# Full attention prepared during the layer norm, its first operands split by VectorE; the local blocks' residual added sequence by sequence

## The chip, the cores and the metric

The kernel runs on one core of a Trainium2 chip, in one launch. The metric is the device time of the launch in microseconds, lower is better, and the median of several runs is compared. The engines are TensorE (PE: matmuls, with its weight loads shown as PEld), VectorE (DVE), ScalarE (ACT), GpSimd (POOL) and SyncE (SP, which issues most transfers here). TensorE has a granted clock with two levels, 1.2 and 2.4 GHz, which the profile shows as 0.50 and 1.00.

## The reference

The input x has 4 sequences of 512 tokens with 128 features. Two "layers" of a macaron network are applied to it:

```python
x = x + 0.5 * _L0_ffn_ref(_layernorm(x))     # 8 gated experts
x = x + _L0_attn_ref(_layernorm(x))          # linear attention, 16 heads of 64
x = x + 0.5 * _L0_ffn_ref(_layernorm(x))     # the experts again
x = x + 0.5 * _L1_ffn_ref(_layernorm(x))     # 6 x (local attention, window 32; gated feed-forward)
x = x + _L1_attn_ref(_layernorm(x))          # full attention, 16 heads of 8, two sets of keys
x = x + 0.5 * _L1_ffn_ref(_layernorm(x))     # the six local layers again
```

The full attention takes queries, keys, second keys (`W_K_prime`) and values from the normalised x, forms `softmax(q k^T / sqrt(8)) v` for both sets of keys over all 512 tokens of a sequence, and mixes the two results with `alpha` and `1 - alpha` before the output projection. The 0.5 of the fourth and the sixth line is the "residual" of this case: half of what the six local layers give is added to x.

## The kernel before

Everything stays on chip, features on the 128 partitions: `M.x` is [128, 4 x 512]. The program is a sequence of blocks, and the order of instructions within a block is written out by hand for each engine. A block ends with a barrier of all engines (the lines L93 and L502 in the trace), after which the engines branch into the next block. The blocks around the change are, in order: `loc0` (the six local layers), the layer norm `ln4`, the full attention, the layer norm `ln5`, and `loc1` (the six local layers again).

**Local block.** It walks over 96 tiles of 128 tokens (6 layers x 4 sequences x 4 tiles) in a software pipeline: in step `n` each engine works on tiles `n`, `n-1`, ... down to `n-9`, and nine further steps (`for n in range(9): step(DEPTH, n, ...)`) drain it. The feed-forward output of a whole sequence is added to the working copy `zs` in step `n-9` of its last tile by `add_ffn` (L1255 for the lower 64 partitions, L1258 for the upper 64, which are shifted by one token). Of the last layer, sequence 0 is added at step 12 of layer 5, and sequences 1, 2 and 3 at steps 0, 4 and 8 of the drain. `rescale` (L1241) starts the feed-forward of the next sequence. `maximum` (L1205) starts the softmax of a tile. After the drain, VectorE adds `0.5 * zs` to `M.x` in two instructions over all four sequences (L1322, L1324).

**Layer norm.** `layernorm_block` computes means with matmuls against a constant (L107), subtracts (DVE L138), squares (ACT L132), forms the variance (PE L112), takes the inverse square root by a table-free guess and three Newton steps on VectorE (L66 to L75), spreads it by matmuls (L118) and multiplies (DVE L147) into `M.xh`. SyncE and GpSimd have no work in `ln4`.

**Full attention.** It walks over 16 groups `u` (4 sequences x 4 groups of four heads), 16 slots each; `K` counts the slots, and `begins(K, offset)` says whether group `u` has its step of that offset in slot `K`. Ahead of the slots stand: three transfers by SyncE (L1405 to L1407: the weights `wqkk`, `wv_full`, `wo_full`), a memset of `lowest` on GpSimd (L1551), and on VectorE two memsets of `V`, five tiny instructions for the two mixing coefficients, and three instructions that fold signs and the scale into `wqkk` (L1579 to L1593). TensorE and ScalarE wait for all of this. The first slots (K = -16 to -10) then project values (L1457, four matmuls against one PSUM bank) and queries, keys, second keys (L1465) of group 0. Each of these three is copied to `plain` by ScalarE (L1538, L1540), and is split into operands for the fast matmul format: VectorE cuts low bits (`high`, L1610), GpSimd multiplies by a sign column (`rest`, L1559) and adds the two (`qkk`, L1563). There are two buffers of `plain`, `high` and `rest`. In slot K = 0 the score matmuls (L1441) of group 0 start, once all three operands are there (`split_ready`); VectorE reduces each pair of banks to a maximum (L1601).

## Time and profile before

| | |
|---|---|
| time, median of 3 runs | 4337.57 us (4336.9 to 4341.59) |
| the profiled execution, its own time | 4342.59 us |
| its span, first to last instruction | 4340.8 us |
| PE busy | 4033.6 us, 93% |
| DVE busy | 3357.6 us, 77% |
| POOL busy | 2965.1 us, 68% |
| ACT busy | 2587.4 us, 60% |
| `loc0` ends, `ln4` ends, full attention ends | 2186.9, 2206.7, about 2710 us |

A busy share is a mean over the whole span, so it says nothing of a seam between two blocks, where one engine works and the others wait. Such places are read from the timeline: a row has the start, the time in microseconds, the engine, the line, what is written from what, the shapes, and in brackets how long the engine sat idle before and what released it.

### The profile page before, as it was taken

The page shows a single profiled execution, that of the slowest core. Times are in us where ns is not written, and L with a number is a line of the kernel's source. Part 1 is how long each engine was busy: PE and PEld are TensorE (multiplying, and loading weights), DVE is VectorE, ACT ScalarE, POOL GpSimd, SP SyncE. Part 2 cuts the span into 40 slices and gives each one's busy share as a digit, 9 for nine tenths or more (in the row PEclk, how much of TensorE's full clock was granted, in tenths as well). Part 3 has the DMA queues.
Part 4 walks back from the last instruction along what each step waited for, and adds up shares of the span by engine and source line. Part 5 has one row for each costly group of instructions (what it writes and reads, how often), then busy time and mean ns, then how long its engine had stood idle before and what let it go on. Part 6 is the DMA issues. An engine that isn't in the chain of part 4 may idle for free. (4 is left out here: it accounts for less than half of the span.)

```text
span 4340.8 us, 151604 instructions
## 1 busy us (share of the span) xinstructions
PE 4033.6 (93%) x66856; PEld 2965.1 (68%) x66856; DVE 3357.6 (77%) x3997; ACT 2587.4 (60%) x3022; POOL 2965.1 (68%) x3501
## 2 busy tenths in 40 slices
PE   8989969999999999999968888799999999999997
PEld 5655557877777777887633332577877887777775
DVE  5635568887888888888658884689888888887885
ACT  4424436666666667666527775367666666666664
POOL 2202158988888888888524441688888888888884
PEclk9999989999999999999969997899999999999999
DMA  4304233233233323322100000332323333232221
GB/s 150 124 10 143 105 94 82 75 88 82 75 88 80 83 78 84 90 69 74 40 11 1 1 1 1 105 86 78 85 78 85 88 84 87 72 88 78 73 67 38
DMA packets 169726, 316.94 MB, mean 73 GB/s; under 512 B 39336, under 2 KB 43056, under 8 KB 166640
## 3 DMA queue, kind: packets, MB, share of 16 engines
q1 hardware_dynamic: 153520, 241.18, 20.5%
q0 software_dynamic: 15552, 66.07, 4.9%
q8 instruction: 529, 8.67, 0.9%
q14 instruction: 125, 1.02, 0.1%
HBM read 92.03 MB, written 20.05 MB: 26 GB/s over the span
## 5 line engine op out<-in xcount | busy, mean ns | idle before, releaser
L684 PE MATMUL psum<-loc_w_hl,loc_z_lo 128*128 128x512 f32 x1152 | 508.5, 441 | 36.1 <-DMA loc_w_hl<-parted 25.9
L1069 POOL TENSOR_TENSOR loc_rc_k<-loc_rc_k,loc_rs_k 128x1024 f32<-128x1024 f32 x192 | 454.5, 2367 | 18.9 <-DVE loc_rs_k L1197 18.9
L1183 DVE TENSOR_REDUCE loc_ssq<-loc_sq 128x16 f32<-128x1024 f32 x384 | 463.9, 1208 | 3.4 <-POOL loc_rn L1065 3.3
L930 ACT ACTIVATE loc_sq<-psum 128x1024 f32<-128x1024 f32 x192 | 197.0, 1026 | 444.1 <-PE psum L686 439.0
L1069 POOL TENSOR_TENSOR loc_rc_q<-loc_rc_q,loc_rs_q 128x1024 f32<-128x1024 f32 x192 | 459.3, 2392 | 0.0
L686 PE MATMUL psum<-loc_w_hl,loc_z_hi 128*128 128x512 f32 x1152 | 455.3, 395 | 1.8 <-issue 1.8
L685 PE MATMUL psum<-loc_w_hl,loc_z_hi 128*128 128x512 f32 x1152 | 454.3, 394 | 2.5 <-issue 2.5
L1087 POOL TENSOR_TENSOR loc_prob<-loc_prob,loc_recip 128x1024 f32<-128x1024 f32 x192 | 365.9, 1906 | 97.2 <-DVE loc_recip L1220 96.6
L781 PE MATMUL psum<-loc_PT,loc_V 64*64 64x32 f32 x24576 | 404.8, 220 | 10.4 <-issue 10.2
L781 PEld LDWEIGHTS psum<-loc_PT,loc_V 64*64 64x64 f32 x24576 | 381.2, 135 | 35.6 <-issue 12.4
L801 PEld LDWEIGHTS psum<-loc_outT,loc_wo 128*128 128x128 f32 x3072 | 378.5, 194 | 17.8 <-issue 1.5
L1075 POOL TENSOR_TENSOR loc_qk_q<-loc_rc_q,loc_rn 128x1024 f32<-128x1024 f32 x192 | 366.0, 1906 | 27.0 <-issue 1.3
L1178 DVE TENSOR_TENSOR loc_rc_q<-psum,loc_rot 128x1024 f32<-128x1024 f32 x192 | 234.8, 1223 | 193.3 <-ACT loc_sq L925 160.4
L801 PE MATMUL psum<-loc_outT,loc_wo 128*128 128x128 f32 x3072 | 380.2, 278 | 0.0
L1075 POOL TENSOR_TENSOR loc_qk_k<-loc_rc_k,loc_rn 128x1024 f32<-128x1024 f32 x192 | 367.3, 1913 | 12.0
L755 PEld LDWEIGHTS psum<-loc_kT,loc_qT 64*32 64x32 f32 x24576 | 270.7, 105 | 134.5 <-issue 132.7
L960 ACT ACTIVATE loc_PT<-psum 128x1024 f32<-128x1024 f32 x192 | 197.0, 1026 | 260.7 <-PE psum L691 260.7
L755 PE MATMUL psum<-loc_kT,loc_qT 64*32 64x64 f32 x24576 | 310.8, 226 | 43.3 <-issue 42.9
L1522 ACT ACTIVATE full_probT<-psum 128x512 f32<-128x512 f32 x512 | 272.4, 598 | 120.8 <-PE psum L1448 120.8
L384 DVE TENSOR_TENSOR moe_hid<-moe_hid,moe_spread 128x512 f32<-128x512 f32 x256 | 218.3, 869 | 153.5 <-ACT moe_hid L298 142.7
L1601 DVE TENSOR_REDUCE full_least<-psum 128x2 f32<-128x1024 f32 x256 | 305.9, 1219 | 28.9 <-PE psum L1441 23.5
L1205 DVE TENSOR_REDUCE loc_negmax<-psum 128x16 f32<-128x1024 f32 x192 | 234.4, 1221 | 108.5 <-PE psum L755 107.0
(199 smaller groups left out, 9753.3 us busy)
## 6 DMA issues: line engine op xcount, KB each, us to landing
loc_V<-loc_V SPq DMA_DIRECT2D x1152, 128.0 KB
loc_V<-loc_V SPq DMA_DIRECT2D x672, 64.0 KB
loc_w_hl<-parted POOLq DMA_DIRECT2D x72, 512.0 KB, 4.3
parted<-moe_halves POOLq DMA_DIRECT2D x18, 1024.0 KB, 5.2
moe_spread<-moe_gates SPq DMA_DIRECT2D x64, 256.0 KB, 4.1
moe_raw<-in_wqkv POOLq DMA_DIRECT2D x18, 512.0 KB, 6.0
moe_w<-in_moe_w SPq DMA_DIRECT2D x32, 256.0 KB, 3.3
loc_wo<-in_wo SPq DMA_DIRECT2D x12, 512.0 KB, 4.8
```

Of the source, the lines that this page charges most:

```text
L684: pe.matmul(M.bank[bank + g], z_lo[:, r, tokens], w[:, 0, cols], start=True, stop=False)
L685: pe.matmul(M.bank[bank + g], z_hi[:, r, tokens], w[:, 1, cols], start=False, stop=False)
L686: mm = pe.matmul(M.bank[bank + g], z_hi[:, r, tokens], w[:, 0, cols], start=False, stop=True)
L755: mm = pe.matmul(M.bank[YB + c][q:q + 32, p * 64:(p + 1) * 64], qT[r:r + 64, p, q:q + 32], kT[r:r + 64, p, k0:k0 + 64], start=False, stop= ...
L781: mm = pe.matmul(M.bank[WB + c][64 * j:64 * j + 64, m * P + q:m * P + q + 32], V2[r:r + 64, b, w, p * 64:(p + 1) * 64], PT[r:r + 64, p, q: ...
L801: mm = pe.matmul(M.bank[ZB][:, 0:P], wo[:, p, :], outT[:, p // (PAIRS // 2), p % (PAIRS // 2), :], start=(p == 0), stop=(p == PAIRS - 1))
L1069: pool.tensor_tensor(rc, rc, rs[:, :], ALU.add).then_inc(added, 1)
L1075: pool.tensor_tensor(pair_major(out[:, :, :, :]), by_pair(rc), spread_heads(rn[:, a:a + HEADS], DH), ALU.mult).then_inc(ready, 1)
L1087: pool.tensor_tensor(both, both, spread_heads(recip[:, :], 2 * WINDOW), ALU.mult).then_inc(p_ready, 1)
L1183: dve.tensor_reduce(ssq[:, a:a + HEADS], heads(sq[:, :]), AX_X, ALU.add).then_inc(totalled, 1)
L1522: act.activation(probT[:, (u * 8 + y * 4 + kb) % SETS, r, :], B[B_BANKS[n % 3]], ACT.Exp).then_inc(b_free, 1)
L1601: dve.tensor_reduce(least[:, u % 2, i, 2 * (k % 2):2 * (k % 2) + 2, y], M.psum[:, b:b + 2, :], AX_X, ALU.max, negate=True).then_inc(a_free, 1)
```

## The change

Four things are changed.

1. The three weight transfers, the memsets, the coefficients and the folding of `wqkk` move from the head of the full attention into the layer norm block `ln4` ahead of it: SyncE issues the transfers there, and GpSimd does all the rest (VectorE's part too).
2. The value projection moves from offset `PROJECT - 2` to `PROJECT + 6`, behind the three projections of its group, on TensorE and ScalarE.
3. For group 0 alone, VectorE does GpSimd's two steps of the split (`rest` and the sum) as well; GpSimd splits from group 1 on.
4. In both local blocks the residual is added to `M.x` right behind each sequence's last `add_ffn`, in two instructions of 512 columns for each sequence, instead of two of 2048 columns at the end.

```diff
@@ layernorm_block (called with full=A for ln4)
+        if full is not None:
+            @block.sync
+            def _(sp):
+                sp.dma_start(M.f_wqkk[:, :, :], full["wqkk"].rearrange("p (y n) -> p y n", y=3)).then_inc(M.f_loaded, 16)
+                sp.dma_start(M.f_wv[:, :], full["wv_full"]).then_inc(M.f_loaded, 16)
+                sp.dma_start(M.f_wo[:, :], full["wo_full"]).then_inc(M.f_loaded, 16)
+
+            @block.gpsimd
+            def _(pool):
+                pool.wait_ge(M.full_loaded, 16 * M.full_dmas)
+                pool.tensor_scalar(M.f_other[:, :], M.sel[:, SUM_ROW:SUM_ROW + 1], -1.0, 1.0, ALU.mult, ALU.add).then_inc(M.f_folded, 1)
...
+                pool.memset(M.f_lowest[:, :, :, :], 0.0).then_inc(M.f_prepared, 1)
+                pool.memset(M.f_V[:, :, :, :, AD + 1:32], 0.0).then_inc(M.f_prepared, 1)
+                pool.memset(M.f_V[:, :, :, :, AD:AD + 1], 1.0).then_inc(M.f_prepared, 1)
...
+                pool.wait_ge(M.f_loaded, 48)
+                for y, cols, factor in ((0, slice(0, 2 * AD), AD ** -0.5), (0, slice(2 * AD, 3 * AD), -AD ** -0.5),
+                                        (slice(1, 3), slice(AD, 2 * AD), -1.0)):
...
+                    pool.tensor_scalar(w, w, factor, None, ALU.mult).then_inc(M.f_prepared, 1)
+                pool.wait_ge(M.f_prepared, 7)
@@ local block, add_ffn
+                if L * SEQS + s >= (DEPTH - 1) * SEQS:
+                    x_out = M.x[:, r * T:(r + 1) * T]
+                    dve.wait_ge(z_ffn, upto_seq(L, s))
+                    dve.scalar_tensor_tensor(out=x_out[0:64], in0=zs[0:64, r, 0:T], scalar=0.5, in1=x_out[0:64],
+                                             op0=ALU.mult, op1=ALU.add)
+                    dve.scalar_tensor_tensor(out=x_out[64:P], in0=zs[64:P, r, 1:T + 1], scalar=0.5, in1=x_out[64:P],
+                                             op0=ALU.mult, op1=ALU.add).then_inc(x_added, 1)
@@ local block, behind the drain
-            dve.wait_ge(z_ffn, upto_seq(DEPTH, -1))
-            x_out = M.x[:, :].rearrange("p (s n) -> p s n", n=T)
-            dve.scalar_tensor_tensor(out=x_out[0:64], in0=zs[0:64, :, 0:T], scalar=0.5, in1=x_out[0:64],
-                                     op0=ALU.mult, op1=ALU.add)
-            dve.scalar_tensor_tensor(out=x_out[64:P], in0=zs[64:P, :, 1:T + 1], scalar=0.5, in1=x_out[64:P],
-                                     op0=ALU.mult, op1=ALU.add).then_inc(x_added, 1)
@@ full_attention_block, schedule and PE, ACT
-    FIRST, LAST = PROJECT - 2, SLOTS * GROUPS + OUT - SLOTS + 1
+    FIRST, LAST = PROJECT, SLOTS * GROUPS + OUT - SLOTS + 1
-            u = begins(K, PROJECT - 2)
+            u = begins(K, PROJECT + 6)
-            pe.wait_ge(M.full_loaded, 16 * M.full_dmas)
-            pe.wait_ge(prepared, 6)
-            pe.wait_ge(v_loaded, 16)
-            pe.wait_ge(out_loaded, 16)
@@ full_attention_block, gpsimd
-            pool.memset(lowest[:, :, :, :], 0.0).then_inc(prepared, 1)
-                    if u is not None:
+                    if u:
@@ full_attention_block, vector (the memsets, coefficients and folds at its head are gone)
                         dve.tensor_scalar(high[:, m % 2, :].bitcast(I32), plain[:, m % 2, :].bitcast(I32), LOW_BITS, None,
                                           ALU.bitwise_and).then_inc(cut, 1)
+                        if u == 0:
+                            sign = SIGNS + (y > 0)
+                            dve.tensor_scalar(rest[:, m % 2, :], plain[:, m % 2, :], M.sel[:, sign:sign + 1], None,
+                                              ALU.mult).then_inc(parted, 1)
+                            dve.wait_ge(cut, m + 1)
+                            dve.wait_ge(parted, m + 1)
+                            dve.tensor_tensor(qkk[:, u % KEPT, y, :], high[:, m % 2, :], rest[:, m % 2, :],
+                                              ALU.add).then_inc(split_ready, 1)
```

What stands on VectorE between the end of `ln4` (the last two branches) and the first score maximum (`full_least`), before the change:

```order
L147 TENSOR_TENSOR xh_late<-xh_late,psum 128x512 x4
L93 UNCONDITIONAL_BRANCH
L1576 UNCONDITIONAL_BRANCH
L1579 MEMSET full_V 128x128x23
L1580 MEMSET full_V 128x128
...
L1593 TENSOR_SCALAR full_wqkk<-full_wqkk 128x16x16
L1593 TENSOR_SCALAR full_wqkk<-full_wqkk 128x16x8
L1593 TENSOR_SCALAR full_wqkk<-full_wqkk 128x32x8
L1610 TENSOR_SCALAR full_high<-full_plain 128x512 x3
L1601 TENSOR_REDUCE full_least<-psum 128x2 x4
```

and with the change (line numbers are those of the changed kernel):

```order
L178 TENSOR_TENSOR xh_late<-xh_late,psum 128x512 x4
L93 UNCONDITIONAL_BRANCH
L1597 UNCONDITIONAL_BRANCH
L1614 TENSOR_SCALAR full_high<-full_plain 128x512
L1618 TENSOR_SCALAR full_rest<-full_plain,sel 128x512
L1622 TENSOR_TENSOR full_qkk<-full_high,full_rest 128x512
...
L1605 TENSOR_REDUCE full_least<-psum 128x2 x4
```

(the three rows of the split stand there three times). The preparation is gone from the head of the block, and six instructions have come into the split. The preparation stands now on GpSimd, between the end of `loc0` and the end of `ln4`, where it had no instruction before:

```order
L137 UNCONDITIONAL_BRANCH
L140 TENSOR_SCALAR full_other<-sel 128x1
...
L143 MEMSET full_lowest 128x1024
L144 MEMSET full_V 128x128x23
L145 MEMSET full_V 128x128
...
L156 TENSOR_SCALAR full_wqkk<-full_wqkk 128x16x16
L156 TENSOR_SCALAR full_wqkk<-full_wqkk 128x16x8
L156 TENSOR_SCALAR full_wqkk<-full_wqkk 128x32x8
L93 UNCONDITIONAL_BRANCH
L93 ISA
```

The end of a local block on VectorE, here of `loc1`, from sequence 2's `add_ffn` (its two instructions write `zs`) to the end, before the change:

```order
L1255 SCALAR_TENSOR_TENSOR zs<-psum,loc_vec,zs 64x512
L1258 SCALAR_TENSOR_TENSOR zs<-psum,loc_vec,zs 64x512
L1241 TENSOR_TENSOR loc_xn<-loc_xc,psum 128x512
L1248 SCALAR_TENSOR_TENSOR loc_gg<-psum,loc_vec,loc_gg 128x512 x2
...
L1258 SCALAR_TENSOR_TENSOR zs<-psum,loc_vec,zs 64x512
L1322 SCALAR_TENSOR_TENSOR x<-zs,x 64x2048
L1324 SCALAR_TENSOR_TENSOR x<-zs,x 64x2048
```

and with the change:

```order
L1286 SCALAR_TENSOR_TENSOR zs<-psum,loc_vec,zs 64x512
L1289 SCALAR_TENSOR_TENSOR zs<-psum,loc_vec,zs 64x512
L1295 SCALAR_TENSOR_TENSOR x<-zs,x 64x512
L1297 SCALAR_TENSOR_TENSOR x<-zs,x 64x512
L1272 TENSOR_TENSOR loc_xn<-loc_xc,psum 128x512
L1279 SCALAR_TENSOR_TENSOR loc_gg<-psum,loc_vec,loc_gg 128x512 x2
```

Sequence 2's residual stands now ahead of `loc_xn`, which starts sequence 3's feed-forward; the two wide instructions at the end are replaced by two such narrow ones for sequence 3.

## Rows read from the trace of the kernel before

**Rows 1.** Timeline from the end of `loc0` to the first scores.
```profile
2182.28 2.28 DVE L1322 SCALAR_TENSOR_TENSOR x<-zs,x 64x2048 f32<-64x2048 f32 x1
2184.57 2.29 DVE L1324 SCALAR_TENSOR_TENSOR x<-zs,x 64x2048 f32<-64x2048 f32 x1
2188.09 5.38 PE L107 MATMUL psum<-x,mean_w 128*128 128x512 f32 x8 [7.40 <-PEq L502]
...
2197.20 0.17 DVE L68 TENSOR_SCALAR ln_rstd<-ln_var 128x16 int32<-128x16 int32 x1
...
2205.97 0.69 DVE L147 TENSOR_TENSOR xh_late<-xh_late,psum 128x512 f32<-128x512 f32 x1 [0.45 <-PE psum L118]
2207.37 0.34 SPq L1405 DMA_DIRECT2D full_wqkk<-in_wqkk  x1
2207.37 0.95 POOL L1551 MEMSET full_lowest<- 128x1024 f32 x1 [43.66 <-POOLq L93]
...
2208.05 2.51 DVE L1579 MEMSET full_V<- 128x2944 f32 x1 [1.40 <-PEq L93]
...
2213.35 2.05 PE L1457 MATMUL psum<-full_wv,xh_late 128*128 128x128 f32 x8 [7.42 <-DMA full_wo<-in_wo_full]
...
2215.19 4.55 PE L1465 MATMUL psum<-xh_late,full_wqkk 128*128 128x512 f32 x6
...
2217.14 0.60 ACT L1538 ACTIVATE full_plain<-psum 128x512 f32<-128x512 f32 x1 [1.02 <-PE psum L1465]
...
2217.84 1.82 POOL L1559 TENSOR_SCALAR full_rest<-full_plain,sel 128x512 f32<-128x512 f32 x1 [9.52 <-ACT full_plain L1538]
2217.85 0.45 DVE L1610 TENSOR_SCALAR full_high<-full_plain 128x512 int32<-128x512 int32 x1 [4.79 <-ACT full_plain L1538]
...
2225.79 1.26 POOL L1563 TENSOR_TENSOR full_qkk<-full_high,full_rest 128x512 fp32r<-128x512 f32 x1
...
2227.11 0.80 PE L1441 MATMUL psum<-full_qkk 32*128 32x512 f32 x4 [7.37 <-POOL full_qkk L1563]
```

**Rows 2.** Timeline and stages (windows) where the expert block follows `ln2`.
```profile
332.07 0.69 DVE L147 TENSOR_TENSOR xh_early<-xh_early,psum 128x512 f32<-128x512 f32 x1 [0.43 <-PE psum L118]
...
333.51 3.59 PE L262 MATMUL psum<-xh_early,wg 128*8 128x512 f32 x8 [1.48 <-PEq L93]
...
333.00:338.00 5.00, 3.59 (x8) 0.66 (x8) 1.97 (x4) 1.71 (x3) 2.30 (x2) 1.00 0.64 203
```

**Rows 3.** Windows: us, busy (count) of PE, PEld, DVE, ACT, POOL; granted clock; DMA share, GB/s.
```profile
2208.00:2209.00 1.00, 0.00 (x0) 0.00 (x0) 0.95 (x1) 0.00 (x0) 0.32 (x1) 0.80 0.79 113
...
2265.00:2270.00 5.00, 4.41 (x28) 1.40 (x24) 4.02 (x5) 3.07 (x7) 1.70 (x2) 0.84 0.02 3
...
2300.00:2320.00 20.00, 18.74 (x122) 7.30 (x116) 17.05 (x21) 15.52 (x31) 10.08 (x8) 1.00 0.00 1
```

**Rows 4.** Single lines: durations min/median/max in ns, first and last start.
```profile
L384 DVE TENSOR_TENSOR moe_hid<-moe_hid,moe_spread x256: 675/692/2818, 45.8 to 536.8; 128x512 f32<-128x512 f32 x128
L1188 DVE TENSOR_SCALAR loc_ssq<-loc_ssq x192: 169/676/2046, 587.6 to 4265.1; 128x32 f32<-128x32 f32 x192
```

**Rows 5.** Timeline of the drain of `loc1`.
```profile
4279.94 0.76 DVE L1258 SCALAR_TENSOR_TENSOR zs<-psum,loc_vec,zs 64x512 f32<-64x512 f32 x1
...
4281.90 1.22 DVE L1205 TENSOR_REDUCE loc_negmax<-psum 128x16 f32<-128x1024 f32 x1 [1.21 <-PE psum L755]
...
4312.72 0.76 DVE L1258 SCALAR_TENSOR_TENSOR zs<-psum,loc_vec,zs 64x512 f32<-64x512 f32 x1
4313.51 0.69 DVE L1241 TENSOR_TENSOR loc_xn<-loc_xc,psum 128x512 f32<-128x512 f32 x1
```

**Rows 6.** Sequence 0's `add_ffn` in `loc1`: timeline and a window.
```profile
4219.88 1.23 DVE L1197 TENSOR_TENSOR loc_rs_q<-psum,loc_rot 128x1024 f32<-128x1024 f32 x1
...
4231.33 1.23 DVE L1178 TENSOR_TENSOR loc_rc_q<-psum,loc_rot 128x1024 f32<-128x1024 f32 x1 [1.52 <-ACT loc_sq L925]
...
4204.00:4268.00 64.00, 63.43 (x1339) 51.77 (x1340) 53.79 (x65) 43.72 (x44) 53.57 (x67) 1.00 0.27 72
```

More of the change, by code:

```diff
@@ L87, in stage_semaphores, with layernorm_block @@
     return sem
-def layernorm_block(nc, M, src, dst, name, shifted=None):
+def layernorm_block(nc, M, src, dst, name, shifted=None, full=None):
     WIDE = 32
@@ L1319, in _, with full_tensors, full_attention_block @@
                 step(DEPTH, n, lambda t: t < 0)
-            dve.wait_ge(z_ffn, upto_seq(DEPTH, -1))
-            x_out = M.x[:, :].rearrange("p (s n) -> p s n", n=T)
-            dve.scalar_tensor_tensor(out=x_out[0:64], in0=zs[0:64, :, 0:T], scalar=0.5, in1=x_out[0:64],
-                                     op0=ALU.mult, op1=ALU.add)
-            dve.scalar_tensor_tensor(out=x_out[64:P], in0=zs[64:P, :, 1:T + 1], scalar=0.5, in1=x_out[64:P],
-                                     op0=ALU.mult, op1=ALU.add).then_inc(x_added, 1)
-def full_attention_block(nc, M, W):
+def full_tensors(nc, ctx, M):
+    sb = lambda n, s: ctx.enter_context(nc.sbuf_tensor(f"full_{n}", s, F32))
+    sem = lambda n: ctx.enter_context(nc.semaphore(f"early_{n}"))
+    M.f_coefs, M.f_other = sb("coefs", [P, 2]), sb("other", [P, 1])
+    M.f_wqkk = sb("wqkk", [P, 3, 4 * P])
+    M.f_wv, M.f_wo = sb("wv", [P, D]), sb("wo", [P, 4 * D])
+    M.f_lowest = sb("lowest", [P, 2, TILES, P])
+    M.f_V = sb("V", [P, 2, TILES, AH, 32])
+    M.f_loaded, M.f_prepared, M.f_folded = (sem(n) for n in ("loaded", "prepared", "folded"))
+def full_attention_block(nc, M):
     GROUPS = 4 * SEQS
@@ L1333, in full_attention_block @@
     PROJECT = -14
[L1334 removed]
+    FIRST, LAST = PROJECT, SLOTS * GROUPS + OUT - SLOTS + 1
     SETS, KEPT = 4, 4
[L1336 removed]
+    HI, SELECTED, SIGNS = 3 * AD, 0, 2
     with ExitStack() as ctx:
@@ L1450, in _ @@
                                   skip_group_check=True).then_inc(b_full, 1)
-                u = begins(K, PROJECT - 2)
+                u = begins(K, PROJECT + 6)
                 if u is not None and u % 4 == 0:
@@ L1522, in _ @@
                         act.activation(probT[:, (u * 8 + y * 4 + kb) % SETS, r, :], B[B_BANKS[n % 3]], ACT.Exp).then_inc(b_free, 1)
-                u = begins(K, PROJECT - 2)
+                u = begins(K, PROJECT + 6)
                 if u is not None and u % 4 == 0:
@@ L1720, in program @@
             M.xh = late.enter_context(nc.sbuf_tensor("xh_late", [P, NTOK], F32))
-            layernorm_block(nc, M, M.x, M.xh, "ln4")
-            full_attention_block(nc, M, A)
+            with ExitStack() as wide:
+                full_tensors(nc, wide, M)
+                layernorm_block(nc, M, M.x, M.xh, "ln4", full=A)
+                full_attention_block(nc, M)
             layernorm_block(nc, M, M.x, M.xh, "ln5", M.zs)
```

53 lines of the change are left out of this document (14 added, 39 removed).

## The prediction

> **What bounds the kernel now.** The change touches two kinds of seam, so I read the timeline there first, then the waits, then the stages around them. At the head of the full attention [rows 1] every engine waits for one chain. `ln4` ends with VectorE's L147 at 2205.97 + 0.69 = 2206.66. Weights are asked for at 2207.37 and the last of them releases TensorE only at 2213.35. The value projection takes TensorE until 2215.19, when the query projection starts; ScalarE has its result at 2217.14. Then the split of three operands runs through GpSimd, 1.82 us for the first product and 1.26 us for the last sum, and the first score matmul starts at 2227.11. Between end of `ln4` and first scores lie 20.45 us, and TensorE idles for 7.42 and 7.37 of them. Nothing comes into this stage from outside afterwards: all sixteen groups follow from group 0, so what group 0 gains the whole stage gains.
>
> The second seam is the end of each local block: the last `add_ffn` is followed by two instructions of 2.28 and 2.29 us, from 2182.28 to 2186.86 = 4.58 us, with no other engine at work, and `ln4` begins behind them [rows 1]. It is there twice.
>
> **The change, part by part.**
>
> *Preparation moved into `ln4`.* SyncE's transfers start about 20 us earlier. They took 2213.35 - 2207.37 = 5.98 us from the first issue to the last landing [rows 1]; `ln4` lasts from 2186.86 to 2206.66 = 19.8 us, so they are hidden. GpSimd gets a memset of 1024 columns (0.95 us, the row of L1551), one of 2944 (VectorE took 2.51; at GpSimd's rate of 1024 in 0.95 it is 2.7), a small one, five tiny ones, and behind the landed weights three products of 256, 128 and 256 columns. At the rate of L1559, 1.82 for 512, these are together 2.3 us. Sum: start at about 2187.6, tiny ones and memsets until 2193, weights there at 2193.5, products until about 2196. It ends 10 us ahead of `ln4`'s end and 1 us ahead of the Newton chain (L68 at 2197.20). Cost: nothing. If that cover were gone, each of the three products could hold up a VectorE instruction by its own length, 0.9 us at most.
>
> *TensorE's start.* With nothing to wait for but the barrier, it begins as it does where the expert block follows `ln2` [rows 2]: L147 ends at 332.76 and the matmul starts at 333.51, 0.75 us later. The seam behind `loc0` gives the other bound: 2186.86 to 2188.09, 1.23 us. I take 0.75, since the block ahead is the same layer norm: start at 2207.41 on the clock of the old trace, against 2215.19, so 7.78 us earlier. The value projection that stood ahead of it goes behind and fills part of a wait.
>
> *Clock.* At 2207.41 the clock is still granted in full: in 2208 to 2209 it reads 0.80, and TensorE had been idle since 2206 [rows 3]. Where `ln2` hands over in the same way the clock reads 1.00 from 333 to 338, and eight matmul records took 3.59 us, 0.45 each [rows 2]. A projection is two records, so the first is ready after 2 x 0.45 + 0.2 of latency = 1.1 us in place of 2217.14 - 2215.19 = 1.95. Were the clock at its lower level, it would be 1.95 again; both are kept.
>
> *The split on VectorE.* ScalarE copies in 0.60; VectorE starts 0.11 later (2217.85 against 2217.74). It then needs for each of three operands `high` 0.45, `rest`, and the sum. `rest` is a one-operand instruction of 512 columns like `high`: 0.45, or 0.69 if it runs at the rate of L147; I take 0.45. The sum has two SBUF operands, median 0.69 [rows 4]. With 0.05 for the waits on its own results that is 1.6 per operand. ScalarE's copies of the second and third operand are hidden behind it: the projections come every 0.9 us. Sum: 1.1 + 0.6 + 0.11 + 3 x 1.6 + 0.06 = 6.7 us from the start of the query projection to the first scores, where it was 2227.11 - 2215.19 = 11.92. Gain 5.2 us. With the lower clock 0.85 to 1.1 less (the third projection then comes after 5.2 us); with the slower `rest` 0.7 less.
>
> So the first scores start at 2214.1 in place of 2227.11: **13.0 us** earlier. Bounds: 13.0 - 1.1 - 0.7 - 0.5 (barrier) = 10.7, and 13.3 if the two-step instructions overlap their ends. The value projections of sequences 1 to 3 move by eight slots within the running stage; the work is the same, and I set them at nothing, with half a microsecond either way each.
>
> L1188, a VectorE instruction of 32 columns, has a least time of 169 ns and a median of 676 [rows 4], so VectorE does wait for something beside a working GpSimd. The Trainium skill (SBUF — State Buffer, Who interferes with whom) names it: a VectorE instruction in a two-port mode, or with two SBUF operands while GpSimd reads SBUF, takes a shared port in turns with GpSimd, the later one waiting for the whole instruction. That rule speaks against the preparation in `ln4`. By it the three products could each hold up one Newton step if they came 1 us later than worked out, and the sum would be 2.7 us less.
>
> *The residual.* Four pairs of 64x512 replace one pair of 64x2048. One instruction costs 0.69 us by the two-operand row [rows 4], a pair 1.4 with its wait. I place each pair:
> - Sequence 3: it is all that is left at the end. 4.58 - 1.4 = 3.2 us gained.
> - Sequence 2: in the drain, L1258 ends at 4313.48 and `rescale` L1241 starts at 4313.51, with no idle time; everything to the end hangs on it [rows 5]. The pair now stands between them. 1.4 us lost.
> - Sequence 1: L1258 ends at 4280.70 and VectorE idles 1.21 us until TensorE's scores let L1205 start at 4281.90 [rows 5]. The pair fits but for 0.2 us, and that softmax has slack. Nothing; 1.4 if the cover is gone.
> - Sequence 0: in the full pipeline, ahead of L1197 at 4219.88. VectorE's next idle time, 1.52 us ahead of L1178 at 4231.33, absorbs 1.4; TensorE is busy 63.43 of 64 us there, so it sets the pace and VectorE has slack [rows 6]. Nothing; 1.4 if not.
>
> Net 3.2 - 1.4 = 1.8 us per block, **3.6 us** for both; bounds 0.8 (sequence 0 exposed in both) and 4.0.
>
> **Sum.** 13.0 + 3.6 = 16.6 us. On the profiled execution's own time, 4342.59, that is 4326.0. That execution is 5.0 us above the median of the runs, so against the median: 4337.57 - 16.6 = 4321.0, or 0.38% less. Bounds of the terms alone: 10.7 + 0.8 = 11.5 and 13.3 + 4.0 = 17.3 us, that is 4326.1 to 4320.3; with the 2 us by which three runs' medians may differ (their own spread is 4.7), 4328 to 4318.
>
> **The rivals.** A difference within 0.2%, 8.7 us, is about what a measurement of this kernel can't tell from none.
>
> *The clock carries over.* The projections of group 1 run among group 0's first slots, at the lower level. TensorE will now idle for only about 3 us ahead of the first scores (from the end of the value projection, 2207.4 + 2.7 + 1.1 = 2211.2, to 2214.1), in place of 7.37. If the clock survives that, three projections take 1.1 in place of 1.95 each, in slots where TensorE had no idle time: 2.6 us more, and if it stays up until the old rise in 2265 to 2270 [rows 3], a few more. Time: 4321.0 - 2.6 to - 6 = 4315 to 4318.4. Against it: in 2208 to 2209 the full level was lost after an idle time of this length. For it: more work now lies close together ahead of the gap.
>
> *A wait takes the place of the one removed.* TensorE's new start is in a block whose code no engine has run yet; VectorE's first instruction in that block came only at 2208.05, 1.39 us behind L147, while SyncE and GpSimd had begun at 2207.37 [rows 1]. If every engine pays something of this kind, or the preparation disturbs `ln4`, or sequence 0's pair costs both blocks 1.4 us, 4 to 8 us of the gain are lost: 4325 to 4329.
>
> *It doesn't do what it says.* The operands come earlier, but the gain is less than 8.7 us: that needs the split on VectorE to take 4 us more than worked out, as if each `rest` or sum ran at more than twice its row's median. The two-operand row has a maximum of 2818 ns, yet that was beside a working GpSimd, which is idle here. Time: 4329 to 4338.
>
> *Slower.* The one mechanism that is large enough is the clock of the full attention's body. At the full level TensorE is busy 18.74 of 20 us [rows 3]; the same work at the lower level would take up to 37.5, so each microsecond at the lower level costs up to 0.47. The rise in 2265 to 2270 came when TensorE had hardly idle time. Were it delayed by a disturbance in the new order (the value projections now stand in the middle of a group), the change would be slower from 16.6 / 0.47 = 35 us more at the lower level on, and clearly so from 54: 4346 or more. Nothing speaks for a delay of this length, since the order of the first 35 slots is otherwise the same.
>
> **How the numbers follow.** Forecast 0.62; clock carried over 0.13; a wait in its place 0.13; doesn't do what it says 0.08; slower 0.04. The predicted time is the forecast's, 4321.0. For 8 in 10 the range takes the first three with their ends: 4315 to 4329. Faster by over 0.2% are the first three but for the last edge of the third, 0.86; within 0.2%, 0.11; slower by over 0.2%, 0.03.
>
> **What would show it.** Right: the first query projection within 1.3 us of L147's end, at the full clock; no wait for `full_wo`; first scores 7 to 8 us behind `ln4`'s end (20.45 before); GpSimd's last weight product over 8 us ahead of that end; one pair of `x<-zs,x` 64x512 at the end of each local block, 1.4 us long, and one directly ahead of `loc_xn` of sequence 3; sequence 0's pair with TensorE's busy share unchanged. Wrong: an idle time of TensorE of over 1.5 us behind the barrier; `ln4` longer than 19.8 us; VectorE's split beyond 5.5 us; a rise of the clock in the full attention more than 45 us behind its first scores (2227 to 2266 before), which would cost, or less than 30, which would give.

## The result, and the profile after

The changed kernel takes 4303.62 us (median of 6 runs, 4293.63 to 4315.7) beside 4338.4 for the kernel before on the same chip (6 runs, 4332.78 to 4346.0): ratio 0.9927, 95% interval 0.9906 to 0.9949. A second job gave 0.9939 (0.9918 to 0.9960). On 4337.57 these are 31.7 and 26.5 us, so about 29 us in place of the 16.6 predicted (the two medians of the first job lie 34.8 us apart, within its interval), and the time lies below the range. The profiled execution's own time is 4293.63 us, the fastest of the six, its span 4291.8.

The head of the full attention in the timeline of the changed kernel, against [rows 1]; columns as there:

```profile
2168.35 0.43 SPq L134 DMA_DIRECT2D full_wv<-in_wv_full  x1
2169.31 2.55 POOL L144 MEMSET full_V<- 128x2944 f32 x1
2173.85 2.29 POOL L156 TENSOR_SCALAR full_wqkk<-full_wqkk 128x256 f32<-128x256 f32 x3 [1.38 <-DMA full_wo<-in_wo_full]
2177.11 0.17 DVE L68 TENSOR_SCALAR ln_rstd<-ln_var 128x16 int32<-128x16 int32 x1
2184.53 0.69 DVE L178 TENSOR_TENSOR xh_late<-xh_late,psum 128x512 f32<-128x512 f32 x1 [0.20 <-PE psum L118]
2185.98 2.81 PE L1489 MATMUL psum<-xh_late,full_wqkk 128*128 128x512 f32 x6 [1.48 <-PEq L93]
2187.11 0.60 ACT L1560 ACTIVATE full_plain<-psum 128x512 f32<-128x512 f32 x1 [12.34 <-PE psum L1489]
2187.74 0.43 DVE L1614 TENSOR_SCALAR full_high<-full_plain 128x512 int32<-128x512 int32 x1 [2.52 <-ACT full_plain L1560]
2188.08 0.48 DVE L1618 TENSOR_SCALAR full_rest<-full_plain,sel 128x512 f32<-128x512 f32 x1
2188.63 1.05 PE L1481 MATMUL psum<-full_wv,xh_late 128*128 128x128 f32 x8
2188.67 0.69 DVE L1622 TENSOR_TENSOR full_qkk<-full_high,full_rest 128x512 fp32r<-128x512 f32 x1
...
2191.74 0.69 DVE L1622 TENSOR_TENSOR full_qkk<-full_high,full_rest 128x512 fp32r<-128x512 f32 x1
2192.48 0.80 PE L1465 MATMUL psum<-full_qkk 32*128 32x512 f32 x4 [2.80 <-DVE full_qkk L1622]
2193.32 1.23 DVE L1605 TENSOR_REDUCE full_least<-psum 128x2 f32<-128x1024 f32 x1 [0.89 <-PE psum L1465]
```

The reader is to see that every step stands where it was put. The weights land inside `ln4`, and GpSimd's last product ends at 2176.14. VectorE's chain of small instructions starts 0.8 us later (L66 at 2176.90), and the first Newton instruction shown (L68) still takes 0.17. `ln4` ends at 2185.22, the first query projection starts 0.76 behind it, six matmul records take 2.81 (0.47 each), and the first scores come 7.26 us behind `ln4`'s end, where it was 20.45. The seam gives 13.2 us; 13.0 was predicted.

The windows from the first maximum (L1605, L1601 before) to the first output, and from there to the last output of the full attention, of the changed kernel, then of the kernel before; columns as in [rows 3]:

```profile
2193.32:2262.40 69.08, 56.31 (x288) 20.03 (x288) 61.41 (x64) 36.42 (x67) 28.24 (x20) 0.86 0.00 0
2262.40:2660.80 398.40, 347.94 (x2226) 127.81 (x2226) 305.66 (x333) 279.96 (x527) 140.34 (x102) 0.97 0.00 1
```

```profile
2227.95:2302.40 74.45, 62.63 (x288) 21.63 (x288) 62.51 (x65) 36.69 (x67) 28.20 (x20) 0.74 0.00 1
2302.40:2706.30 403.90, 354.50 (x2226) 129.40 (x2226) 305.43 (x333) 279.94 (x527) 139.85 (x102) 0.95 0.00 1
```

The counts are the same and VectorE, ScalarE and GpSimd are as long busy, yet the stretches are 5.4 and 5.5 us shorter. What differs is the granted clock. It has two levels, 1.2 and 2.4 GHz, so 0.74 over 74.45 us is 2 x 0.26 x 74.45 = 39 us at the lower one; 0.86 over 69.08 us is 19 by the same sum, and 20 when added up over windows of 2 us, as all such times below. In the second stretch it is 44 and 25 us, in the changed kernel all of it in the drain behind the last scores. This is what the prediction's sum has no term for. Windows of the changed kernel around the place where the level comes back to stay:

```profile
2189.00:2193.00 4.00, 1.20 (x11) 0.78 (x9) 3.21 (x7) 1.17 (x2) 0.00 (x0) 0.94 0.01 2
2193.00:2198.00 5.00, 3.69 (x12) 1.08 (x8) 3.49 (x3) 0.57 (x1) 0.00 (x0) 0.50 0.00 0
...
2218.00:2221.00 3.00, 2.85 (x12) 1.46 (x11) 1.80 (x3) 2.27 (x3) 1.57 (x1) 0.70 0.00 0
2221.00:2226.00 5.00, 4.53 (x28) 1.50 (x26) 5.00 (x7) 4.80 (x10) 4.23 (x4) 1.00 0.00 0
```

The level falls with the first scores: 0.94 up to 2193, then 0.50. It comes back once, falls again, and rises for good 27 to 28 us behind the first scores (2192.48), where it was 39 to 41 ([rows 3] against 2227.11).

The last rows of VectorE in `loc1`, against [rows 5]:

```profile
4264.69 0.74 DVE L1286 SCALAR_TENSOR_TENSOR zs<-psum,loc_vec,zs 64x512 f32<-64x512 f32 x1 [2.94 <-PE psum L889]
4265.45 0.76 DVE L1289 SCALAR_TENSOR_TENSOR zs<-psum,loc_vec,zs 64x512 f32<-64x512 f32 x1
4266.25 0.68 DVE L1295 SCALAR_TENSOR_TENSOR x<-zs,x 64x512 f32<-64x512 f32 x1
4266.94 0.69 DVE L1297 SCALAR_TENSOR_TENSOR x<-zs,x 64x512 f32<-64x512 f32 x1
4267.66 0.69 DVE L1272 TENSOR_TENSOR loc_xn<-loc_xc,psum 128x512 f32<-128x512 f32 x1
```

Sequence 2's pair stands ahead of `rescale`, with no idle time between, for 1.4 us, as predicted. The last pair of the block takes 1.42 where 4.58 stood.

The two profiled executions are 48.0 us apart at VectorE's last instruction. The full attention (end of `ln4` to last output) has 499.7 - 475.6 = 24.1 of them, and the other 24 lie in everything else, where only 3 to 4 were expected. So one pair of profiles doesn't tell what the change is worth; the experiments had to.

### The profile page after: what moved, and what is told of

Read it like the earlier page. It is cut to its first block and busy times, and to the rows that moved or that the text cites. A ratio compares the mean times of both kernels' runs of the same rounds, so it can differ in the third digit from the quotient of the medians.

```text
span 4291.8 us, 151611 instructions
## 1 busy us (share of the span) xinstructions
PE 4005.3 (93%) x66856; PEld 2945.8 (69%) x66856; DVE 3375.6 (79%) x4005; ACT 2587.5 (60%) x3022; POOL 2963.9 (69%) x3505
## 5 line engine op out<-in xcount | busy, mean ns | idle before, releaser
L1605 DVE TENSOR_REDUCE full_least<-psum 128x2 f32<-128x1024 f32 x256 | 305.9, 1219 | 19.9 <-PE psum L1465 15.1
```

Source lines behind the costliest of these rows:

```text
L1605: dve.tensor_reduce(least[:, u % 2, i, 2 * (k % 2):2 * (k % 2) + 2, y], M.psum[:, b:b + 2, :], AX_X, ALU.max, negate=True).then_inc(a_free, 1)
```

## The experiments

The expectations below come from another count of the time at the lower level: their 46 (or 45), 34 and 20.5 us behind the first maximum are 39, 28 and 20 in the windows of the profile, their 95 and 58 for the full attention 98 and 60.

Each job shares its runs of the kernel before. Its median was 4338.4, 4336.6, 4325.8, 4334.9, 4327.2 and 4329.6 us from job to job, and in the four jobs with 23 runs or more of it the middle 8 in 10 of the 122 single runs went from 4320 to 4345. Times are therefore read as ratios within a job; a ratio of 0.9977 is 10 us.

**The parts, and both kernels again.** `resid_only` has the per-sequence residual alone, `full_only` the preparation, the moved value projection and the split on VectorE, with the old residual.

> The kernel before once more, unedited. Ratio 1.000. Its profile tells how far the local layers and the first linear stages move from one execution to the next, and whether the lower clock in the first 39 us of the full attention (2227 to 2266) is there every time: theory B says yes, theory A has no view.

> The changed kernel once more, unedited, for its own spread. Its median beside the kernel before is asked first: theory A (only the seams changed: 16.6 us) puts it near 4321 and the measured 4303.6 down to luck of the runs; theory B (the seams plus something systematic) near 4304. In its profile the first scores should again start 7.3 us behind the end of the layer norm. Where the profiles of two runs of one kernel differ in stages that the edit doesn't touch, that difference belongs to the run.

> The kernel before with the residual alone added sequence by sequence. Prediction's sum: 3.6 us less (ratio 0.9992), bounds 0.8 to 4.0. Rival: the residual's pairs change the running pipeline of the local blocks and give the unexplained rest, some 18 us (ratio 0.995).

> The changed kernel with the old residual at the end of each local block: preparation in the layer norm, value projection behind, split on VectorE. Prediction's sum: 13.0 us less (ratio 0.997). Rival, the clock: with an earlier rise in the full attention 18 to 28 us less (ratio 0.9935 to 0.996). If the residual carries the rest, 13.

| | median us | ratio | 95% interval |
|---|---|---|---|
| before_again | 4335.55 | 1.0003 | 0.9982 to 1.0024 |
| after_again | 4310.56 | 0.9939 | 0.9918 to 0.9960 |
| resid_only | 4319.83 | 0.9964 | 0.9944 to 0.9984 |
| full_only | 4311.46 | 0.9942 | 0.9923 to 0.9961 |

Each part gives about 12 us more than its seams (15.6 and 25 in place of 2 to 3.6 and 13), and the two don't add up. Runs list a granted clock: on average 0.9700 before and 0.9739 to 0.9751 in the edited kernels, which is 260 us of a run at the lower level against 215 to 225.

**Is it any edit at all?** `null_start` and `null_ln4` change something that no seam can show; `resid_again` repeats `resid_only`; `prep_only` has the preparation alone: it keeps the value projection ahead, the split on GpSimd and the old residual.

```diff
 null_start
-                    dve.memset(M.mean_w[:, :], 1.0 / D).then_inc(consts, 1)
+                    dve.memset(M.mean_w[:, 0:64], 1.0 / D)
+                    dve.memset(M.mean_w[:, 64:P], 1.0 / D).then_inc(consts, 1)
 null_ln4
...
+                pool.memset(M.zs[:, :, 0:1], 0.0).then_inc(opened, 1)
```

> The kernel before, but the memset of the 128 columns of mean_w at the very start is written as two of 64 columns: one more VectorE instruction (under 0.1 us, beside loads that take longer), and no other difference; ln4, the full attention and the local blocks are as before. So far the three edited kernels (residual alone, full attention's head alone, both) each gained 11 to 13 us more than what their seams show, and all of it went with 35 to 45 us less at TensorE's lower clock. Theory A (the edits themselves set how long the clock stays at its lower level): this kernel is as before, 4336 within 4 us (ratio 0.999 to 1.001), with about 260 us at the lower level per run. Theory B (any change to the program re-deals how the clock's drops fall, the unchanged text having drawn a bad hand): this kernel gains as well, 4322 to 4328, with about 225 us at the lower level.

> The kernel before, with one small GpSimd memset (4 columns, into the padding of zs that nobody reads by then) added to ln4, where GpSimd has nothing else to do. No seam changes. Theory A (the edits themselves move the clock): as before, 4336 within 4 us. Theory B (any change re-deals it): 4322 to 4328. A third outcome, this one gains and the memset at the start doesn't: then something in ln4 or behind it (GpSimd's first work there) would matter, and the seam would have to show a difference.

> The kernel with the residual alone, run once more as it was. Its seams give about 2 us (3.2 gained at each block's end, 2.2 lost in front of sequence 3's rescale), and it measured 4319.83 beside 4336.63, 16 us less, with 225 us at the lower level in place of 260. If that is a property of the kernel: 4318 to 4323 beside 4336 again. If it was the chip's luck in that job: 4330 to 4335.

> The preparation alone: weights, memsets, coefficients and weight products in ln4, the old order of the value projection (ahead of the first query projection), the split of group 0 on GpSimd, the old residual. By the terms of the sum it gains the earlier start of TensorE less the value projection that stays ahead: value projection at ln4's end + 0.75, 1.85 long, so the first query projection 2.6 us behind ln4's end in place of 8.5, that is 5.9 us earlier; the split takes its 11.9 us as before, or 11 where the clock is still up. First scores 13.7 to 14.5 us behind ln4's end (20.45 before). Seam gain 6 to 7 us. Theory A with the clock following the seams: 4336 - 6.5 - 12 = 4317 to 4319; seams alone: 4329 to 4331.

Ratios 0.9997 (0.9983 to 1.0011) and 0.9997 (0.9982 to 1.0011) for the two null edits: theory B of the expectations, by which any edit at all re-deals the clock to a gain, falls. `resid_again` has 0.9976 (0.9960 to 0.9993), 10 us, and `prep_only` 0.9961 (0.9947 to 0.9975), 17 us, where its seam is 21.2 - 13.4 = 7.8 us.

**Clock up by added work, and the pieces left.** `after_warm` and `before_warm` add matmuls that nobody reads; `no_split` leaves group 0's split to GpSimd; `late_pair` moves the residual pairs behind the next sequence's `rescale`.

```diff
 after_warm (before_warm: FILL is 7)
+    FILL, SMALL = 3, 2
...
+                if K == 0:
+                    for _ in range(FILL):
+                        pe.matmul(B[PV], M.ident[:, :], M.xh[:, 0:T], start=True, stop=True, skip_group_check=True)
+                if 0 <= K < VALUES - 1:
+                    for _ in range(1 if K < 7 else SMALL):
+                        pe.matmul(B[PV][:, 0:P], M.ident[:, :], M.xh[:, 0:P], start=True, stop=True, skip_group_check=True)
 late_pair
...
                     rescale(L, n - 6)
+                    s = (n - 6) // TILES - 1
+                    if L * SEQS + s >= (DEPTH - 1) * SEQS:
+                        add_residual(L, s)
```

> The changed kernel with each sequence's residual pair moved behind the next sequence's rescale (the last pair stays where it is). In the profiles so far sequence 2's pair stands directly ahead of that rescale and the time from add_ffn of sequence 2 to that of sequence 3 is 18.5 to 18.6 us in both blocks, against 16.2 to 16.4 before. Theory: the pair lies on the path and costs 2.2 us per block. Moved, it lies in an idle time of VectorE of 7.6 us: 16.3 us again, 4.4 us less than the changed kernel, ratio to before about 0.001 lower than the changed kernel's 0.9939. Rival: the 2.2 us are TensorE's lower clock in the drain and stay: 18.5 us again.

> The changed kernel with matmuls added whose result nobody reads, where TensorE idles at the head of the full attention: three of 512 columns ahead of the first scores and one or two of 128 columns in each of the first 22 slots. Clock theory (what the prediction left out is time at TensorE's lower clock in the full attention's head, 20.5 us of it now, 34 to 46 before, at 0.2 to 0.37 us each): the first 70 us behind the first scores show under 10 us at the lower level, first maximum to first output takes 66 to 67.5 us (69.1 now), and the kernel is 2 to 5 us faster than the changed one. Rival (the head is bound by ScalarE and VectorE and the clock there only keeps company): the level is up and the stage stays at 69 us or grows by the added matmuls, up to 2 us.

> The kernel before with the same added matmuls (seven of 512 columns ahead of the first scores, where it waits longer for the split). Its profiles show 45 us at the lower level behind the first maximum in three of four and 34 in one, and 33 or 14 us in the drain. Clock theory: under 15 us at the lower level in the first 70 us, first maximum to first output 66 to 69 us (74.4 or 70.3 now), and if the drain follows the head, its stage 396 rather than 404 us: 6 to 15 us faster than before (ratio 0.9965 to 0.9986), without any of the change. Rival (the gain beyond the seams is not clock): within 2 us of before.

> The changed kernel, but with group 0 split on GpSimd as before. By the terms: VectorE's split 3 x 1.54 us, GpSimd's 1.82 and 1.26 for one and three of these in a pipeline, so the first scores should come 3.5 to 4.5 us later (11 to 12 us behind ln4's end in place of 7.26). Seams alone: 4 us slower than the changed kernel (ratio to before about 0.995). If the longer idle time of TensorE ahead of the first scores also keeps the clock down longer, as the clock theory would allow, 5 to 10 us slower, with 30 us or more at the lower level in the 70 us behind the first maximum.

| | median us | ratio | 95% interval |
|---|---|---|---|
| late_pair | 4314.2 | 0.9954 | 0.9936 to 0.9973 |
| after_warm | 4318.67 | 0.9965 | 0.9950 to 0.9979 |
| before_warm | 4342.72 | 1.0023 | 1.0006 to 1.0041 |
| no_split | 4324.33 | 0.9976 | 0.9963 to 0.9988 |

The same first window (first maximum to first output) in `no_split`, then in `after_warm`:

```profile
2204.96:2288.20 83.24, 72.16 (x288) 23.75 (x288) 62.64 (x65) 36.76 (x67) 28.14 (x20) 0.62 0.00 0
```

```profile
2212.38:2279.80 67.42, 61.63 (x358) 27.78 (x358) 61.53 (x64) 36.48 (x67) 28.24 (x20) 1.00 0.00 1
```

`no_split` shows what a later head can cost behind it. Its first maximum comes 12.5 us behind `ln4`'s end in place of 8.1, 4.4 us as expected; the same 288 matmul records behind it then take 83.24 us at clock 0.62 (63 us at the lower level) in place of 69.08 at 0.86 (20). That is 14.2 us for 43 us more at the lower level, 0.33 each, and against the changed kernel's two ratios (0.9927, 0.9939) it is 16 to 21 us slower in all. The same instructions give the same order without any edit near them: the two profiles of the kernel before differ here too, and the second one reads

```profile
2224.70:2295.03 70.33, 58.25 (x288) 20.54 (x288) 61.70 (x65) 36.39 (x67) 28.23 (x20) 0.80 0.00 1
```

(28 us at the lower level) where the first took 74.45 at 0.74 (39). `after_warm` gives the other end: at 1.00 the stretch takes 67.42, so full clock gained only 1.7 us, net of whatever the 70 added matmul records cost in it. The price is not one rate: from 20 to 28 us at the lower level it is 1.2 us, from 28 to 39 it is 4.1, from 39 to 63 it is 8.8. That VectorE, with 61 to 63 us busy in every row, sets the pace at the cheap end and TensorE at the dear one is the likely reason; it was not tested by itself.

How late the head is doesn't decide the clock alone. `prep_only`'s first maximum comes 13.4 us behind `ln4`'s end, later than in `no_split`, and yet it has 19 us at the lower level behind it and takes 69.1 us. What decides when the level comes back is not shown.

The added matmuls don't pay. In `after_warm` the stage came out as expected, but the kernel is 11 to 16 us slower than the changed one, where 2 to 5 us less were expected. `before_warm`'s full attention takes 486.4 us, 9.4 less than the old code's mean below, but the kernel is 10 us slower than before, where 6 to 15 us less were expected. The loss is in code that wasn't touched: between the last output and the first `add_ffn` of `loc1` it takes 236.0 us, against 224.2 to 227.0 in every kernel without added matmuls (229.6 in `after_warm`). The local scores (L755) of the whole kernel in `before_warm`, then in `before_again`, by what ended the idle time of TensorE's matmuls and weight loads ahead of them and who waited for them:

```profile
  issue: 185.8, 284
...
  DVE loc_negmax L1205: 110.6, 106
```

```profile
  issue: 161.6, 276
...
  DVE loc_negmax L1205: 91.8, 99
```

"Issue" is time in which an engine waited for nothing that the profile shows. The view adds up two streams that overlap, the matmuls' own (47.1 and 35.6 us of it) and that of their weight loads, PEld (138.7 and 125.9). These scores are 256 small matmuls with a weight load each, per tile, and the kernel with the added instructions ahead of them has 12 us more of it in front of the matmuls, 13 in front of the loads, and 19 more of VectorE's waiting. Over the sixteen uncut profiles of this study the time outside the full attention (3807 to 3845 us) goes with the sum of the weight loads' "issue" idle time (699 to 744 us), at about 0.75 us per us and with 4 us of scatter. It is a correlation, and much of that idle time lies beside running matmuls: the matmuls themselves have 45 to 62 us of "issue" and 271 to 292 us of idle time of every kind. The Trainium skill (Runtime: NRT & Kernel Launch, Instruction fetch mechanics) says that the sequencer refills the instruction buffer while the page before it runs and that this is mostly hidden; no run here shows what these idle times consist of.

`late_pair` does what it says: VectorE's rows in its `loc1`:

```profile
4281.02 0.76 DVE L1289 SCALAR_TENSOR_TENSOR zs<-psum,loc_vec,zs 64x512 f32<-64x512 f32 x1
4281.81 0.69 DVE L1272 TENSOR_TENSOR loc_xn<-loc_xc,psum 128x512 f32<-128x512 f32 x1
4282.42 0.68 DVE L1299 SCALAR_TENSOR_TENSOR x<-zs,x 64x512 f32<-64x512 f32 x1
```

`rescale` starts 1.4 us earlier, and still nothing is to be seen in the time. From sequence 1's `add_ffn` to the block's end the old residual takes 54.0 us (16 blocks, 52.3 to 54.8), the new one 52.6 (14 blocks, 50.6 to 54.9), `late_pair` 52.2 and 52.9. Identical code differs there by 2 to 4 us with the clock of the drain, in which TensorE has little to do. It doesn't beat the changed kernel. The value of 2.2 us that its expectation states came from four such pairs and was clock as well.

**Cut kernels.** To see the clock's part without the local layers, each local block has 2 of its 6 layers here (four layers of each are left out).

```diff
 def local_transformer_block(nc, M, W, name):
...
+    DEPTH = 2
```

> The kernel before with each local block cut from 6 layers to 2 (four layers of each left out), so that the stages around the change are all there, and the local layers, whose time differs by 10 us and more from one execution to the next in identical code, weigh a third. It is the base for the three kernels beside it: about 4335 less 8 layers of 256 us, 2280 to 2300 us, with a spread between executions under 10 us. If the spread comes from the local layers it falls to about a third of the 22 us (middle 8 in 10) of the long kernel; if from the clock in the full attention, it stays at 12 us or more.

> The changed kernel, cut in the same way. In the profiles of the whole kernels the full attention (end of ln4 to its last output) took 499.7, 486.9, 499.8 and 498.3 us with the old head and 475.6, 475.6, 473.9 and 481.3 with the new one. Seams alone: 13.2 + 2 to 3.6 = 15 to 17 us less than short_before. With the clock: 13.2 + 6 to 9 more in the full attention + 2 to 3.6 = 21 to 26 us less. If the 28 us of the long kernels comes back whole, 27 to 30 less, then nothing of it was in the local layers.

> The residual alone, cut in the same way. Seams alone: 2 to 3.6 us less than short_before. If it also deals the head of the full attention the better clock (58 us at the lower level in the full attention in two profiles of two, against 92 to 95 in three of four before), 10 to 12 us less. If the 12 to 15 us seen in the long kernels came from the local layers, it shrinks to a third: 4 to 5.

> The full attention's head alone (preparation, moved value projection, split on VectorE), old residual, cut in the same way. Seams alone: 13 us less than short_before. With the clock as in the profiles (473.9 against 496.2 on average): 19 to 23 us less. If it is additive with the residual, short_after is lower by short_resid's gain; if both only move the clock to its better course, short_after is lower by 2 to 4 us.

Medians: 2260.33 (5 runs, 2247.94 to 2269.6), 2254.25 (4 runs), 2261.02 (4) and 2252.2 (4). The base was expected at 2280 to 2300 us with a spread under 10; it spans 22, so the spread is not the local layers' alone. Gains of 6, -1 and 8 us, each with a standard error of some 5 us: that excludes the 27 to 30 and 21 to 26 that were asked for, but not the seams alone (15 to 17 for both changes). In the cut kernel before, the full attention took 483.1 us, with 52 at the lower level, in the changed one 478.9 with 55. Over all their runs it is 227 us at the lower level in the cut kernel before and 225 in the cut changed one, so here the change brings no less of it. The cut kernels' heads and drains draw another course of the clock, and there the old code draws a good one: `short_resid`, with the old head, has 69.0 us and 20 at the lower level behind the first maximum. The extra gain seems to hang on what stands around the edit; so few runs don't show more.

**Which residual?** `resid_loc0` changes only the block ahead of the full attention, `resid_loc1` only the one behind it.

```diff
+                if name == "loc0" and L * SEQS + s >= (DEPTH - 1) * SEQS:   (or "loc1")
...
```

> The kernel before with the residual added sequence by sequence in the first local block alone, the one ahead of ln4 and the full attention. Seam: 1.6 to 1.8 us. If the 12 us of resid_only came from the full attention's clock (its head lies at another place behind the block's last matmuls), this kernel has nearly all of it: 8 to 12 us faster than before (ratio 0.9972 to 0.9982), with 58 to 61 us at the lower level between ln4's end and the last output (92 to 95 in three of four profiles before). If the 12 us were from something else, 2 to 6 us.

> The same in the second local block alone, behind the full attention. It cannot touch the full attention, so its seam is all it can give: 1.6 to 1.8 us (ratio 0.9996), the full attention as before (498 to 500 us in most executions). If it gains 6 us or more, the clock of the full attention is not where resid_only's gain came from.

Ratios 0.9991 (0.9975 to 1.0008) and 1.0003 (0.9986 to 1.0020). The order is as the theory wants, the size is not: 4 us and nothing, in place of 8 to 12 and under 2. Both together give less than the 13 us (mean of 0.9964 and 0.9976) of the residual in both blocks, though the intervals of the two reach to 11 and 6 us.

## Why the prediction was wrong

The full attention, in us, of the uncut profiles without added matmuls (end of `ln4` to first maximum; to first output; to last output; in brackets the time at the lower clock in the second and third):

| kernel | head | to first output | to last output | all |
|---|---|---|---|---|
| before | 21.3 | 74.4 (39) | 404.0 (44) | 499.7 |
| null_start | 21.3 | 74.4 (39) | 404.1 (44) | 499.8 |
| null_ln4 | 21.1 | 74.4 (39) | 402.7 (39) | 498.3 |
| resid_loc1 | 21.1 | 74.4 (39) | 398.9 (28) | 494.4 |
| before_again | 20.9 | 70.3 (28) | 395.7 (19) | 486.9 |
| resid_only | 21.0 | 70.3 (28) | 395.7 (19) | 487.1 |
| resid_again | 20.8 | 70.4 (28) | 398.1 (25) | 489.3 |
| resid_loc0 | 20.8 | 70.4 (28) | 404.0 (44) | 495.1 |
| no_split | 12.5 | 83.2 (63) | 397.0 (21) | 492.7 |
| prep_only | 13.4 | 69.1 (19) | 392.3 (9) | 474.9 |
| full_only | 7.8 | 71.7 (31) | 394.4 (15) | 473.9 |
| after | 8.1 | 69.1 (20) | 398.4 (25) | 475.6 |
| after_again | 8.1 | 69.1 (20) | 398.4 (25) | 475.5 |
| late_pair | 8.0 | 69.1 (20) | 404.2 (44) | 481.3 |

- *The step that failed* is the term that the sum doesn't have: the clock behind the first scores. The prediction let the rest of the stage cost what it cost before, "all sixteen groups follow from group 0, so what group 0 gains the whole stage gains", and put a clock that comes back at another time aside with the words "the order of the first 35 slots is otherwise the same". The order was the same, and the stage was not. With the old head, and the old residual ahead of it, four of five profiles have 39 us at 1.2 GHz behind the first maximum and one 28; with the new head it is 20 in three of four, and 31 in one. The full attention's means are 495.8 and 476.6 us: 19.2 less, 13.2 from the seam and 6.0 behind the first maximum, 3.8 of them up to the first output and 2.2 in the rest. The 6.0 has a standard error of 3 us with so few profiles.
- The rival *the clock carries over* had the right term and put it at 2.6 to 6 us, with 0.13; but its way didn't come true. The level did not survive the wait of 2.8 us ahead of the first scores, it fell with them (at 2192.5), and the first projections of group 1 ran at the lower level. What changed is how soon it comes back to stay, under 30 us behind the first scores, which is the mark the prediction gave for a gain. And its time, 4315 to 4318.4, lies above what was measured as well.
- *TensorE's start and the split*: right. 0.76 behind `ln4`'s end (0.75 predicted), projections 0.47 per record (0.45), 1.54 us per operand (1.6), 7.26 in all (7.4), and so 13.2 us (13.0).
- *Preparation in `ln4`*: right in cost, nothing. GpSimd ended 0.8 us ahead of VectorE's chain (1 predicted, from L68) and 9.1 ahead of `ln4`'s end (10 predicted). `ln4` took 18.44 us here and 19.79 before, but that is not the change: over the uncut profiles it goes from 18.4 to 20.3, and `prep_only` and `full_only`, which have the preparation too, take 19.95 and 19.74. The Trainium skill's rule on the shared port (SBUF — State Buffer, Who interferes with whom) was not put to the test: GpSimd was done before VectorE's chain began.
- *The residual*: 3.2 gained and 1.4 lost at the places named. Over the drains it is 54.0 - 52.6 = 1.4 us per block, 2.8 for both, with 0.4 of doubt per block (3.6 predicted).
- *The sum's base*: I let three runs' medians differ by 2 us. From job to job the kernel before differs by 13. The sum was held against one execution of a kernel whose own time goes from 4307 to 4362 in 122 runs.

With what was measured in the profiles the sum is 13.2 + 6.0 + 2.8 = 22.0 us, against 29 from the two ratios, whose intervals reach down to 22 and 17. From 4337.57 that sum would still give 4315.6, just inside the stated range; so some 7 us more have to be found. One profile per kernel can't show them. Outside the full attention the changed code's three profiles take 3815.7 us on average, and the four with the old code there (`before`, `before_again` and the two null edits) 3823.9, with 3807 to 3835 among those four alone.

The granted clock of every single run says more. Within each kernel (260 runs, without those with added matmuls) the time follows the time at the lower level, twice (1 - granted clock) of the run, at 0.39 us per us, and with that taken off the scatter of the runs falls from 8.3 to 5.1 us. This gives an estimate for each kernel: its seams from the profiles, plus 0.39 of the time at the lower level that it has less than the kernel before of the same job. Left out of that time is what the shorter head itself saves (15.4 us at the lower level between `ln4`'s end and the first maximum with the old head, 0.8 with the new one), since the seam has it already.

| kernel | seams | less at the lower level | estimate | measured |
|---|---|---|---|---|
| after_again | 16.0 | 30 | 28 | 26 |
| full_only | 13.2 | 28 | 24 | 25 |
| prep_only | 7.8 | 29 | 19 | 17 |
| resid_only | 2.8 | 35 | 16 | 16 |
| resid_again | 2.8 | 24 | 12 | 10 |
| late_pair | 16.0 | 15 | 22 | 20 |
| no_split | 11.5 | -11 | 7 | 10 |
| resid_loc0 | 1.4 | 10 | 5 | 4 |
| resid_loc1 | 1.4 | -10 | -3 | -1 |
| null_start | 0 | 3 | 1 | 1 |
| null_ln4 | 0 | 5 | 2 | 1 |

So the missing term is about 12 us, of which the full attention's profiles show 6, and the seams with it come to the measured gain of every kernel within some 3 us. The two kernels with added matmuls are the exception: by this sum `after_warm` should gain 30 us and `before_warm` 7; they are 15 and 17 us slower than that, which is what the added matmuls cost. The price of 0.39 is a correlation over runs, and close to the 0.33 of `no_split` and the 0.37 from 28 to 39 us in one stage. Not shown is why one edit draws less time at the lower level than another: the residual in both blocks draws 24 to 35 us less, in either block alone 10 less or 10 more.

## What to carry to other kernels

A change that shortens an idle time of TensorE at the head of a pipeline is worth the seam plus what the clock does behind it: read the granted clock up to the point where it stays at 2.4 GHz, and give that a term of its own, with both signs (`no_split`: 4.4 us later, 14 us longer behind it; `prep_only`: 5.3 us later, and no longer). Where identical code differs by 25 us between executions, take the stages from several profiles before explaining a difference with one pair, hold a sum against ratios within a job, and compare the granted clock over all runs. An experiment that works by adding instructions can pay for them elsewhere, so look at the untouched stages of it too.

## What the runs showed of the hardware

- The clock's lower level cost between 0.16 us per us (from 20 to 28 us at the lower level, 69.1 to 70.3 us) and 0.37 (from 28 to 39, 70.3 to 74.4) in the same 288 matmul records, and 0.39 as the mean over whole runs. The Trainium skill (TensorE: Matmul & The Clock Gate, Part 1) says that the lower level is the default and that activity lifts it; the 1.00 of `after_warm`, whose only difference is more activity, agrees.
- The course of the clock is not fixed by the code: the stage behind the first maximum had 74.4 us in four profiles and 70.3 in a fifth of the same instructions.
- Matmuls added to hold the clock up did so (1.00 in the stage) and by the estimate above still cost 15 to 17 us of the kernel beside what the clock gave back, part of it in local blocks that were not touched (236.0 and 229.6 us where 224.2 to 227.0 stand in the others).
- TensorE's weight loads idle for 699 to 744 us of a run with nothing that the profile shows to wait for, mostly while matmuls run (93% of the span); two profiles of the same kernel differ by 20 us in it (`resid_only` 723, `resid_again` 703).
